# Layer 1 of a two-layer graph network in the other order: adjacency times features first, weights last

## The reference: what is computed

```python
h = relu(layernorm(x))
# layer 0: attention over the adjacency A, then two steps of diffusion
Xw = h @ Wv + bv;  sj = Xw @ aw[:d];  si = Xw @ aw[d:]
e  = leaky_relu(sj[None, :] + si[:, None] + ab)
T  = A * exp(e);   T = T / (rowsum(T) + 1e-12)
H  = h @ Wk[0] + bk[0] + (T h) @ Wk[1] + bk[1] + (T T h) @ Wk[2] + bk[2]
x  = x + relu(H)
# layer 1: normalised adjacency
h  = relu(layernorm(x))
Ah = A + I;  dh = rsqrt(rowsum(Ah))
x  = x + relu((dh * Ah * dh) h W + bias)
```

## Time and profile before

| | |
|---|---|
| time, median of 3 runs | 801.36 us (801.26 to 802.51) |
| the profiled execution | 801.45 us on the device, span of its instructions 799.5 us |
| TensorE busy | 784.4 us, 98% of the span, 6142 matmuls |
| VectorE, ScalarE, GpSimd busy | 80%, 64%, 16% |
| granted TensorE clock | 0.998 of full speed over the span |

### The profile page before, as it was taken

One profiled execution on the slowest core, in us unless ns is written; L12 is line 12 of the kernel. 1 busy time (PEld: TensorE's weight loads), 2 busy tenths in 40 slices (PEclk: granted clock), 3 DMA queues, 4 the chain that ended last, 5 costly groups with the idle time before them and its releaser, 6 DMA issues.

```text
span 799.5 us, 15983 instructions
## 1 busy us (share of the span) xinstructions
PE 784.4 (98%) x6142; PEld 756.0 (95%) x6142; DVE 638.6 (80%) x1544; ACT 515.5 (64%) x987; POOL 129.4 (16%) x120
## 2 busy tenths in 40 slices
PE   8798999999999999999999999999999999999998
PEld 8597999989999899998999999999999999999998
DVE  6985889868897688976989679896798868895676
ACT  3986766757576676666667567665776657667142
POOL 1032010311104111030201402023010220103200
PEclk9999999999999999999999999999999999999999
DMA  7555435843278251772527625284343842356403
GB/s 240 221 156 170 139 117 177 274 144 134 66 224 295 75 171 54 244 258 67 194 70 250 214 73 192 75 297 156 126 140 128 287 127 99 100 182 234 158 9 106
DMA packets 64492, 128.71 MB, mean 161 GB/s; under 512 B 5536, under 2 KB 31520, under 8 KB 64416
## 3 DMA queue, kind: packets, MB, share of 16 engines
q1 hardware_dynamic: 55648, 97.01, 37.1%
q10 hardware_dynamic: 8768, 30.68, 11.5%
HBM read 119.28 MB, written 8.39 MB: 160 GB/s over the span
## 4 chain that ended last, share of the span: by engine, by line
PE 91%; ACT 4%; DVE 4%; issue 1%; DMA 0%; POOL 0%; SPq 0%; DVEq 0%; ACTq 0%
PE acc L1029 22%; PE acc L1031 22%; PE acc L1030 22%; PE da L904 13%; PE db L904 6%; PE tp L896 3%; ACT tg_e L393 1%; PE acc L924 1%; ACT t_hi L407 1%; ACT tg_e L399 1%; DVE h L587 1%; DMA h<-x_dram 0%; DVE g_tmp L677 0%; DVE ht_lo L606 0%; ACT a_raw L424 0%
## 5 line engine op out<-in xcount | busy, mean ns | idle before, releaser
L1029 PE MATMUL acc<-g_hi,t_hi 128*128 128x256 f32 (+1 forms) x1024 | 293.0, 286 | 2.7 <-DVE g_lo L632 2.7
L1031 PE MATMUL acc<-g_hi,t_lo 128*128 128x256 f32 (+1 forms) x1024 | 289.9, 283 | 0.0
L1030 PE MATMUL acc<-g_lo,t_hi 128*128 128x256 f32 x1024 | 288.7, 282 | 0.0
L1029 PEld LDWEIGHTS acc<-g_hi,t_hi 128*128 128x128 f32 x1024 | 193.9, 189 | 3.1 <-issue 3.1
L1030 PEld LDWEIGHTS acc<-g_lo,t_hi 128*128 128x128 f32 x1024 | 194.3, 190 | 0.0
L1031 PEld LDWEIGHTS acc<-g_hi,t_lo 128*128 128x128 f32 x1024 | 194.1, 190 | 0.0
L1029 PE MATMUL acc<-g_hi,a_hi 128*128 128x256 f32 x512 | 145.5, 284 | 0.1
L1030 PE MATMUL acc<-g_lo,a_hi 128*128 128x256 f32 x512 | 144.0, 281 | 0.0
L1031 PE MATMUL acc<-g_hi,a_lo 128*128 128x256 f32 x512 | 144.0, 281 | 0.0
L327 POOL TENSOR_TENSOR g_lo<-g_tmp,g_hi 128x256 fp32r<-128x256 f32 x64 | 60.6, 947 | 353.0 <-ACT g_hi L449 353.0
L393 ACT ACTIVATE tg_e<-si,sij 128x256 f32<-128x256 f32 x256 | 109.4, 501 | 12.9 <-DVE t_lo L657 10.2
(11 more groups left out here) (129 smaller groups left out, 1424.3 us busy)
## 6 DMA issues: line engine op xcount, KB each, us to landing
a_raw<-adj_dram SPq DMA_DIRECT2D x64, 512.0 KB, 4.5
a_raw<-adj_t_dram SPq DMA_DIRECT2D x64, 512.0 KB, 4.9
tg_a<-adj_t_dram ACTq DMA_DIRECT2D x58, 512.0 KB, 4.0
x_res<-x_dram SPq DMA_DIRECT2D x64, 128.0 KB, 3.6
out_dram<-o_tile SPq DMA_DIRECT2D x64, 128.0 KB, 3.0
h<-x_dram SPq DMA_DIRECT2D x7, 1024.0 KB, 5.3
tg_a<-adj_t_dram SPq DMA_DIRECT2D x6, 512.0 KB, 3.5
h<-x_dram SPq DMA_DIRECT2D x4, 256.0 KB, 4.0
```

The lines of the kernel that those rows point to most:

```text
L1029: nc.tensor.matmul(acc[:, s, 0:n], l_hi, r_hi, start=(jt == 0), stop=False)
L1030: nc.tensor.matmul(acc[:, s, 0:D], l_hi, r_lo, start=False, stop=False)
L1031: ins = nc.tensor.matmul(acc[:, s, 0:n], l_lo, r_hi, start=False, stop=(jt == NT - 1))
```

## The change

Layer 1 is computed in the other order. Before, it was Ah (h W); now it is ((Ah h)^T)^T W:

- **features**: ScalarE normalises x1 into a two-slot buffer `tmp`, with relu, and with dh folded into the scale (`moments1` multiplies the variance by the row sum), then rounds it to `hs_hi` (`hs_high`); GpSimd makes `hs_lo` (`hs_split`). No transposes, no relu and split out of PSUM, no `l1_scaled`/`l1_low`.
- **adjacency product** (`layer1_piece`): the features are the stationary operand and a half row block of Ah, 512 columns wide, is the moving one. There are 16 pieces of 6 matmuls. They leave the product transposed in two PSUM banks at a time, first for node tiles 0 to 3 (in `da`), then for 4 to 7 (in `tp`). The host lays the adjacency out for this (`adj_z`).
- **weights product**: each half is rounded and split once (`zt_high`, `zt_low`, 4 copies of 512 columns each in all), and `out_product` makes each output tile of 6 matmuls with `wl`. Tiles 0 to 3 come between the last pieces, tiles 4 to 7 in the next batch's U phase. The last batch has them at its end.
- **outputs** go round four slots `x_o`, of which two are also the residual's `x_res`; `hs_hi` lies in the space of h0.
- **layer 0's normalisation** of h0 moves from VectorE to ScalarE, with relu and a bias `nb0` that VectorE works out; the statistics for batch 1 are taken at the start of the kernel, and three of batch 0's row sums move from the U phase to layer 0's dense products.
- the unit tables are laid out anew for 16 pieces in the place of 8 Z chunks. Of the two loops over the pieces in the diff the first is ScalarE's, the second VectorE's; the tables are asked behind what is shown.

```diff
-    HIGH_V = {1: (0, 1), 5: (2,), 7: (3,)}
-    PROD_V = {0: 1, 3: 2, 5: 3}
+    HIGH_V = {1: (0, 1), 5: (2,)}
+    PROD_V = {0: 1, 3: 2, 5: 3, 7: 4}
...
-    DIAG_Z = {0: 4, 1: 5, 2: 6, 3: 7}
+    DIAG_Z = {6: NT - 2, 9: NT - 1}
+    OUT_Z = {10 + i: i for i in range(HJ)}
+    OUT_U = {1 + i: HJ + i for i in range(HJ)}
...
+            def hs_split(b, t):
+                pool.wait_ge(hs_hi_done, b * NT + t + 1)
+                nc.gpsimd.tensor_tensor(hs_lo[:, t, :], tmp[:, t % 2, :], hs_hi[:, t, :].bitcast(F32),
+                                        ALU.subtract).then_inc(hs_ready, 1)
...
+            def hs_high(b, par, g):
+                act.wait_ge(nb1_ready, b * NG + g + 1)
+                if g > 0:
+                    act.wait_ge(hs_ready, b * NT + 2 * g)
+                for t in (2 * g, 2 * g + 1):
+                    nc.scalar.activation(tmp[:, t % 2, :], p0[:, par, t, :], ACT.Relu, bias=nb1[:, t:t + 1],
+                                         scale=rstd1[:, t:t + 1]).then_inc(h1_ready, 1)
+                for t in (2 * g, 2 * g + 1):
+                    act.wait_ge(h1_ready, b * NT + t + 1)
+                    nc.scalar.copy(hs_hi[:, t, :], tmp[:, t % 2, :]).then_inc(hs_hi_done, 1)
...
+            def zt_high(b, r):
+                for f in range(KD):
...
+                    nc.scalar.copy(zt_hi[:, f, :], zt[r][:, f, :]).then_inc(zt_hi_done, 1)
...
+                for q in range(NP):
+                    if q == NP // 2:
+                        zt_high(b, 0)
+                    if q + 4 < NP:
+                        a_round(b, (q + 4) // 2, q % 2)
+                    if q == 1:
+                        hs_high(b, par, NG - 1)
...
+                for q in range(NP):
+                    if q == NP // 2:
+                        zt_low(b, 0)
+                    if q + 4 < NP:
+                        a_low(b, (q + 4) // 2, q % 2)
+                    if q == 0:
+                        bias1_of(b, NG - 1)
+                    if q - 1 in OUT_Z:
+                        out_chunk(b, par, OUT_Z[q - 1])
...
+            def layer1_piece(b, q):
+                i, h = q // 2, q % 2
+                r, jt = i // HJ, q % NT
+                pe.wait_ge(a_ready[h], b * NT + NT + i + 1)
+                if r == 0:
+                    pe.wait_ge(hs_ready, b * NT + jt + 1)
...
+                for f in range(KD):
+                    l_hi, l_lo = hs_hi[:, jt, f * P:(f + 1) * P], hs_lo[:, jt, f * P:(f + 1) * P]
+                    nc.tensor.matmul(zt[r][:, f, :], l_hi, r_hi, start=(jt == 0), stop=False)
+                    nc.tensor.matmul(zt[r][:, f, :], l_hi, r_lo, start=False, stop=False)
+                    ins = nc.tensor.matmul(zt[r][:, f, :], l_lo, r_hi, start=False, stop=(jt == NT - 1))
...
+            def out_product(b, t):
+                pe.wait_ge(zt_ready, KD * (2 * b + t // HJ + 1))
+                if t >= OB:
+                    pe.wait_ge(z_tmp_done, b * NT + t - OB + 1)
+                c = slice(t % HJ * P, (t % HJ + 1) * P)
+                split_product(out_bank[t % OB], D, [(zt_hi[:, f, c], zt_lo[:, f, c], wl_hi[:, f, :], wl_lo[:, f, :])
+                                                    for f in range(KD)]).then_inc(out_full, 1)
```

More of the change, by code:

```diff
@@ L283, in batch @@
                         load_chunk(b, i)
[L284 to L294, removed]
+                load_chunk(b, RS + 2)
+                load_chunk(b, RS + 3)
+                if left > 0:
+                    rows(b + 1, (0, 1))
+                for g in range(NG):
+                    if left > 1:
+                        load_h0(b + 2, g)
+                    if g < 2 and left > 0:
+                        rows(b + 1, (g + 2,))
+                    if g == 1:
+                        stores(b, 0)
+                        stores(b, 1)
+                    if g == 2:
+                        stores(b, 2)
+                        stores(b, 3)
+            for g in range(NG):
+                load_h0(1, g)
             rows(0, range(RS))
@@ L304, in _ @@
             batch(B - 1, 0)
-            for s in range(2):
-                sp.wait_ge(stored[s], 16 * (B * NT // 2 + 1))
+            for i in range(HJ, NT):
+                stores(B - 1, i)
+            for s in range(OS):
+                sp.wait_ge(stored[s], 16 * (B * NT // OS))
         @block.gpsimd
@@ L332, in batch @@
                     g1_split(b, i)
-                    if i == 4 and not last:
+                    if i == (3 if b > 0 else -1) and not last:
                         power(rstd0, ve0, ve0_ready, b + 1, rstd0_ready)
@@ L458, in after @@
                 def after(t):
+                    if t in (0, 2) and not last:
+                        norm0(b + 1, 2 + t // 2)
+                    for r in FIRST_ROWS_D.get(t, ()) if b == 0 else ():
+                        rows(b, r)
                     if t == 2:
@@ L544, in _ @@
             for b in range(0, B - 3, 2):
[L545 to L548 removed]
+                batch(b, 0, False)
+                batch(b + 1, 1, False)
+            batch(B - 2, 0, False)
+            batch(B - 1, 1, True)
         @block.vector
         def _(dve):
[L554 to L556 removed]
             dve.sem_inc(x1_ready, 2)
@@ L708, in z_chunk @@
-            def z_chunk(b, par, i):
-                s = i % 2
-                dve.wait_ge(acc_full, b * PHASES + 2 * NT + i + 1)
-                nc.vector.scalar_tensor_tensor(out=z_tmp[:, s, :], in0=acc[:, acc_slot(Z_PHASE, i), 0:D], scalar=dh[:, i:i + 1],
+                at = 2 * i % HJ * P
+                for h in range(2):
+                    blk = a_raw[:, i % RS, at + h * (N // 2 + P):at + h * (N // 2 + P) + P]
+                    ins = nc.vector.tensor_tensor(blk, blk, ident[:, :], ALU.add)
@@ new lines, in out_product, with accumulate @@
+            def out_product(b, t):
[5 more added lines that the diff above has]
+                                                    for f in range(KD)]).then_inc(out_full, 1)
+            def accumulate(b, phase, i, read, before, ready, n, rhs):
+                s = acc_slot(phase, i)
+                if i >= AB:
+                    pe.wait_ge(read, b * NT + i - AB + 1)
+                elif phase == V_PHASE:
@@ L1020, in accumulate @@
                     pe.wait_ge(before, b * NT + NT + i - AB + 1)
-                for jt in tiles:
+                elif b > 0:
+                    pe.wait_ge(before, b * NT + i - AB + 1)
+                for jt in range(NT):
                     if ready is not None and i == 0:
                         pe.wait_ge(ready, b * NT + jt + 1)
-                    if lhs is of_a and jt % HJ == 0:
-                        pe.wait_ge(a_ready[jt // HJ], b * NT + NT + i + 1)
-                    l_hi, l_lo = lhs(i, jt)
+                    l_hi, l_lo = t_hi[:, i, jt, :], t_lo[:, i, jt, :]
```

409 lines of the change are left out of this document (196 added, 213 removed).

## The result

| | before | after |
|---|---|---|
| time, median | 801.47 us (801.26 to 802.51, 4 runs) | 787.13 us (786.95 to 787.24, 4 runs) |
| ratio | | 0.9818, 95% interval 0.9801 to 0.9835: 1.8% faster |
| span of the profiled execution | 799.5 us | 784.8 us |

The account below looks back on a forecast made before the run. TensorE's work was taken to bound the kernel, 96.5 us a batch, VectorE nearest behind. From 801.45 us: -14.1 - 4.4 - 2.4 - 1.5 + 2.0 + 6.5 = -13.9, so 787.5 us; 8 times in 10 between 779 and 800.

Parts of the forecast that it names:

- part 7: Z stage: output product 0 waits 0.9 us for VectorE's split of the transposed product, in 7 batches: +6.5 us.
- part 2: Adjacency product: 96 matmuls of 512 columns take 22.4 us a batch, 192 of 256 columns 22.95: -4.4 us.
- part 3: Layer 1: small waits on the transposes' ScalarE and VectorE steps go, some 0.3 us, 8 times: -2.4 us.
- Part 1: Layer 1: the transposes go, 4 groups in each of 8 batches at 0.44 us, with no cover: -14.1 us.
- Part 4: Batch 0: waits for batch 1's late statistics and normalisation go, against a later first U phase: -1.5 us.
- Part 5: End of the kernel: rounding, split, product and four outputs now follow the last piece: +2.0 us.
- Part 6: Work moved between ScalarE, VectorE and GpSimd in V, Z and U: no engine passes TensorE.
- A: Rival: in Z the queues run slightly better, product 0 finds its operands ready, no new wait: 781 us; chance 0.24.
- B: Rival: GpSimd steps beside VectorE's units are caught each time, delaying the last features by 1 us: 794.5 us; chance 0.19.
- C: Rival: the feature chain is longer than V, a wait of about 4.7 us in 7 batches: 814 us; chance 0.11.
- The turning point of 3.0: The new wait in us a batch from which the 20.4 us of gains are used up: 801 us.
- D: Rival: nothing moves, since gains and waits cancel within 0.2%; chance 0.04.

Follow-up runs that it names:

- Experiment 6: The kernel before with layer 1's 16 transposes a batch done twice, the second over the first: 815.63 us, ratio 1.0170.
- experiment 7: experiment 1's kernel with all but each unit's first and last piece written as matmuls of 256 columns instead of 512: 778.34 us, ratio 0.9706.
- experiment 10: experiment 1's kernel with batch 1's statistics, power, bias and first normalization moved from the start-up back into batch 0's U stage: 779.46 us, ratio 0.9720.
- experiment 11: experiment 1's kernel with batch 0's last three row sums moved from layer 0's dense products back into its U stage: 782.68 us, ratio 0.9769.
- experiment 1: The changed kernel with the output products of tiles 0 to 3 one piece later, behind pieces 11 to 14 instead of 10 to 13: 779.21 us, ratio 0.9715.
- experiment 2: The changed kernel with VectorE's split of the transposed product one place earlier, ahead of unit 4's split: 779.56 us, ratio 0.9720.
- Experiment 5: The changed kernel with its output products two pieces earlier, from behind piece 8 instead of 10: 819.75 us, ratio 1.0228.
- Experiment 4: The changed kernel with its output products one piece earlier, from behind piece 9 instead of 10: 801.14 us, ratio 0.9989.
- experiment 9: The changed kernel with GpSimd's split of the features replaced by a fill with zeros that reads no SBUF: 785.74 us, ratio 0.9799.
- experiment 12: experiment 1's kernel with both batch 1's statistics and first normalization and batch 0's row sums back in batch 0's U stage: 783.56 us, ratio 0.9772.
- experiment 3: The changed kernel with output products one piece later and VectorE's split of the transposed product one place earlier: 779.09 us, ratio 0.9717.

## Why the prediction was right

Point by point, by its own parts; the sum of the working was -13.9, and 14.3 us were gained. The mechanism held (transposes gone, one new wait), and so did most prices; that the total came out within 0.4 us is in part luck, since part 7 came out 1.8 us dearer and parts 2 and 3, with small waits elsewhere that were not foreseen, about 2 us better.

**Part 1, transposes, -14.1.** Experiment 6 gives 13.5, and the trace 1.78 us a batch, 14.2. Right.

**Part 2, 512 for 256 columns, -4.4, and part 3, small waits, -2.4.** The sum is about right, the reason of part 2 is wrong. Pieces do start 1.40 us apart, but experiment 7 reaches the same 25.22 us with 256 columns. What Z gained is real. This is Z before, by the same view:

```profile
405.51:430.07 24.56, 24.55 (x207) 24.34 (x206) 21.51 (x40) 16.52 (x30) 0.00 (x0) 1.00 0.47 147
```

Less 1.43 us for the last products with the weights in it, the 192 matmuls took 23.1 us; now they take 22.4 (25.22 less 2.84 for four output products). The 48 products with the weights fell from 6.04 to 5.69 us, summed between starts of the timelines. That is 1.1 us a batch, but each of the two sums before holds the 0.08 us that the first matmul behind a group of transposes takes longer, and part 1's price has these already. So 0.92 a batch are left, 7.4 for the 6.8 of both parts. 0.51 of it are small waits that went (0.24 in the products, 0.27 in Z, where part 3 had some 0.3), and 0.4 the rest, where part 2 had 0.55. The failed step is to put the difference between 2.87 for 24 and 1.40 for 6 down to the shape, when the two come from different stages. Experiment 7 shows that the new order runs as fast with 256 columns; what makes it faster than the old Z by 0.4 us a batch stays open.

One gain stands in no part. In the six middle batches before, TensorE also lost 0.2 us in layer 0's dense products, ahead of a transpose of the logits (0.44 us to the next start where 0.23 is the rule):

```profile
360.67 0.40 PE L904 MATMUL da<-wa_hi,ht_lo 128*128 128x512 f32 x1
361.11 0.32 PE L924 MATMUL acc<-ident,sij 128*128 128x128 f32 x1
```

Now this is gone: by the spacing of starts, that stage's 512-column products and these transposes take 11.65 us for 11.91, so 0.26 a batch and 1.6 in all. With it a middle batch adds up: 1.78 + 0.92 + 0.26 are 2.96, and the periods without the new wait are 93.6 for 96.55.

**Part 4, batch 0, -1.5.** The first period was 5.43 us over the later ones (101.98 and 96.55). Now it is as long as they are, though it lacks their four output products (2.86), so 2.9 over; U starts 0.7 later. That makes -1.8. But the early statistics have no part in it: they shorten the first period by 0.8 us and delay the first U by about as much (experiment 10). Moving the row sums does the work, and this was a duty that the change itself had made: with h0's normalisation on ScalarE the old place costs 3.5 us more (experiment 11).

**Part 5, the tail, +2.0.** The last piece ends at about 776.5, the last output (below) at 782.58: 6.1 us, of which by part 5's count +2.1 are new.

```profile
776.26 0.40 PE L1073 MATMUL tp<-a_hi,hs_lo 128*128 128x512 f32 x1
...
778.06 0.39 PE L969 MATMUL da<-wl_hi,ht_hi 128*128 128x256 f32 x1 [1.40 <-DVE ht_lo L780]
...
782.16 0.42 DVE L795 SCALAR_TENSOR_TENSOR x_o<-x_o,p 128x256 f32<-128x256 f32 x1
```

**Part 6, what lies beside.** ScalarE has 18.1, 22.6 and 15.3 us in V, Z and U for the 19, 19 and 18 foreseen, VectorE 19.5, 23.0 and 19.0 for 20, 19 and 18. Z is fuller by 4 us than the forecast had it, on both, and still nothing but one wait came of it.

**Part 7, the new wait, +6.5** (7 x 0.9 are 6.3)**.** The place, the waker and the length are as walked: 0.92 us on average for 0.9. Its price was higher, 8.3. Without it a period is 1.19 us shorter (94.78 to 93.59), and experiment 1 gains 7.9 us by the medians and 8.3 by the ratios, where the waits sum to 6.4. The difference, about 0.2 each time, is at the wait's ends in the timeline shown above: the matmul before it still counts as busy for 0.16 us after its place of 0.23 is over, and the first one behind it takes 0.22 for 0.12.

Sum as measured: -14.2 - 7.4 - 1.6 - 1.8 + 2.1 + 8.3 = -14.6, for 14.3 by the medians and 14.7 by the spans.

The rivals: A (781, the cover holds) is what one table entry makes of this kernel, experiments 1 and 2; it missed by the order of two instructions. B (794.5) asked for every GpSimd step to be caught, and the splits averaged 0.97 us. C (814) did not come: the last features were 4.7 to 4.9 us into Z and not 8.3, and no piece waited for them. Experiment 5 shows what a wait of that size does all the same: 3.7 us a batch gives 819.75. The turning point of 3.0 lay too high, since the stretches at half clock and the 0.2 us at each wait's ends come on top. Experiment 4 stood at the time of before with waits of 2.3. D (no change) fell with an interval of 0.9801 to 0.9835.

The prediction left open whether VectorE waits for GpSimd too. It does (experiment 9's rows). By the rule of the Trainium skill (SBUF — State Buffer, Who interferes with whom) it should, so the trace agrees with both halves of it. Its price here is small, 1.4 us in the whole kernel, though the two instructions of experiment 9 alone lose some 8 us on VectorE. That VectorE's slack takes up the rest is likely but not shown by itself.

## What to carry to other kernels

Where an in-order engine makes an operand for TensorE, walk each queue up to it with the durations of the trace; here that found a wait of 0.9 us among 26, and moving either side by one place was worth 1% of the time. Test a price per shape in the same stage before adding it to a sum: here the total was right with a wrong reason. And a move that brings work to an engine makes that engine's later instructions late, so the row sums had to move with the normalisation.

## What the runs showed of the hardware

- **A wait of TensorE can cost more than its length.** After waits of 0.8 to 1.0 us the granted clock stayed at 2.4 GHz all seven times. After the seven of 2.2 to 2.4 (experiment 4) it was 1.2 GHz for some 3.4 us twice, after one of 2.36 and one of 2.94 (experiments 11 and 12) as well, and after 3.6 to 3.8 all seven times (experiment 5). Each such stretch loses 1.5 to 1.7 us. What decides between 2.18 with and 2.42 without, or between the two of 2.19, is open.
- **The kernel before has one such stretch** early in the first U stage, behind the wait of 2.67 us at its start; the changed kernel, with the same wait of 2.80, has none in its profile. Of fourteen profiles nine show it there. It costs little in this place, as TensorE there waits for VectorE's evictions anyway when it runs at full clock (three waits, 1.5 us in all, in the changed kernel; one of 0.4 in experiment 1, which has the stretch): the first periods are 93.70 us in experiment 1 and 93.52 and 93.70 in experiments 3 and 2, which have none.
- **VectorE and GpSimd hold each other up** even in tiny instructions: 0.55 us for 0.16 on 128x2 elements when both inputs are read from SBUF, and no change in the statistics, which read one (experiment 9).
